# Last feed-forward layer of a four-layer transformer kernel: another order of the last eight work units, and another order inside the last matrix product

## The reference, cut to what matters

```
for i in range(DEPTH):                                   # DEPTH = 6
    x = attn_layer(shift_tokens(x), Wqkv[i], q_scale[i], k_scale[i], Wo[i]) + x
    x = ffn_layer(shift_tokens(x), ln_g[i], ln_b[i], W1[i], b1[i], W2[i], b2[i]) + x

attn_layer: q, k, v = x @ Wqkv; l2-normalise q and k; rotate both; softmax(8 q k^T) v over
            the own window and the one before it; times Wo
ffn_layer:  a, gate = layernorm(x) @ W1 + b1;  (a * gelu(gate)) @ W2 + b2
...
return x + tanh(g_ffn[3]) * _L3_ffn_ref(layernorm(x), ...)
```

## Time and profile before

| | |
|---|---|
| time, median of 3 runs | 4802.01 us (4800.52 to 4803.77) |
| the profiled execution, its own time | 4805.08 us |
| its span in the profile | 4803.7 us |
| mean granted clock of TensorE | 0.989 |
| busy share: PE, DVE, ACT, POOL | 96%, 75%, 65%, 54% |
| last `qkv` matmul of the program ends | about 4700.8 us |
| last matmul of the program ends | about 4798.8 us |

### The profile page before, as it was taken

How to read it: one execution, slowest core, us unless ns; L and a number is a source line. 1 busy time by engine, 2 the same in 40 slices (tenths; PEclk the granted TensorE clock), 3 DMA queues, 4 the chain that set the end, 5 groups by cost and what they waited for, 6 DMA issues and landing times.

```text
span 4803.7 us, 92378 instructions
## 1 busy us (share of the span) xinstructions
PE 4591.3 (96%) x34598; PEld 2927.6 (61%) x34664; DVE 3584.6 (75%) x6388; ACT 3135.8 (65%) x7744; POOL 2594.6 (54%) x2346
## 2 busy tenths in 40 slices
PE   6999999999999999969999999999999999999998
PEld 2333333334444343337788888888888888888886
DVE  4767766766675857858888887888888888887885
ACT  3666566556455556557777777777777777777773
POOL 3322211212121222148888788787888887887873
PEclk8999999999999999989999999999999999999999
DMA  5323323332222323212111111111111111111110
GB/s 121 66 50 62 75 42 60 71 63 47 57 40 60 68 41 74 40 34 54 41 41 35 41 40 36 42 39 37 39 44 39 39 36 41 40 36 38 39 44 31
DMA packets 178924, 233.05 MB, mean 49 GB/s; under 512 B 29648, under 2 KB 121424, under 8 KB 178256
## 3 DMA queue, kind: packets, MB, share of 16 engines
q1 hardware_dynamic: 178480, 227.14, 21.0%
HBM read 150.09 MB, written 32.51 MB: 38 GB/s over the span
## 4 chain that ended last, share of the span: by engine, by line
PE 66%; DVE 12%; ACT 8%; POOL 7%; issue 5%; DMA 1%; SPq 0%; another core or an unknown queue 0%; DVEq 0%; ACTq 0%; POOLq 0%
PE psum L1449 13%; PE psum L1493 11%; PE psum L541 5%; PE psum L527 5%; PE psum L506 5%; PE psum L1535 3%; PE psum L1501 3%; PE psum L488 2%; DVE maxes L731 2%; PE psum L1516 2%; PE psum L1525 2%; POOL stats L1818 2%; PE psum L530 2%; ACT lprobs L1760 2%; PE psum L496 2%
## 5 line engine op out<-in xcount | busy, mean ns | idle before, releaser
L941 ACT ACTIVATE probs<-psum 128x1024 f32<-128x1024 f32 x610 | 621.6, 1023 | 449.2 <-PE psum L527 259.7
L731 DVE TENSOR_REDUCE maxes<-psum 128x1 f32<-128x1024 f32 x512 | 618.1, 1216 | 278.0 <-PE psum L506 274.2
L1818 POOL TENSOR_TENSOR stats<-stats,minus_half 128x8 f32<-128x8 f32 x384 | 687.6, 1791 | 32.0
L1760 ACT ACTIVATE lprobs<-psum,small_stats,stats 128x128 f32<-128x128 f32 x1536 | 690.3, 480 | 20.9 <-DVE small_stats L1649 19.9
L1493 PE MATMUL psum<-wqkv_hi,xs_hi 128*128 128x512 f32 (+1 forms) x1536 | 546.6, 356 | 16.4 <-POOL xs_lo L1805 15.2
L1814 POOL TENSOR_TENSOR lwork<-lwork 128x512 f32<-128x512 f32 x384 | 505.1, 1315 | 74.7 <-DVE lwork L1633 74.6
L527 PE MATMUL psum<-stack 98*128 98x512 bf16 x1536 | 502.8, 384 | 25.9 <-DVE maxes L731 12.2
L1493 PE MATMUL psum<-wqkv_lo,xs_hi 128*128 128x512 f32 (+1 forms) x1536 | 519.3, 338 | 0.0
L1493 PE MATMUL psum<-wqkv_hi,xs_lo 128*128 128x512 f32 (+1 forms) x1536 | 519.0, 338 | 0.0
L506 PE MATMUL psum<-stack 96*128 96x512 bf16 x1536 | 473.3, 385 | 33.2 <-ACT probs L938 10.0
L728 DVE CUSTOM_DVE_ANT_0 psum<-psum,mask_by_query 128x1024 f32<-128x1024 f32 x256 | 314.8, 1231 | 217.8 <-PE psum L506 216.2
(11 more groups left out here) (244 smaller groups left out, 11398.0 us busy)
## 6 DMA issues: line engine op xcount, KB each, us to landing
mixed_vals<-vals SPq DMA_DIRECT2D x672, 64.0 KB, 2.0
stack<-k_parts SPq DMA_DIRECT2D x288, 128.0 KB
staged<-in_quads SPq DMA_DIRECT2D x144, 256.0 KB, 3.0
k_parts<-parts SPq DMA_DIRECT2D x48, 384.0 KB, 2.9
stack<-q_parts SPq DMA_DIRECT2D x288, 64.0 KB
staged<-in_w SPq DMA_DIRECT2D x54, 256.0 KB, 3.0
ctx<-in_ctxT SPq DMA_DIRECT2D x24, 512.0 KB, 5.2
q_parts<-parts SPq DMA_DIRECT2D x24, 384.0 KB, 3.2
```

What stands on the lines that cost most here:

```text
L731: ins = vector.tensor_reduce(to, pair(("M", u)), AX.XY, ALU.max)
L941: scalar.activation(probs[:, i % 6, :, :], pair(("E", u)), ACT.Exp).then_inc(S_["E_act"], 1)
L1760: ins = scalar.activation(pr[:, h, :], scores(u)[:, h % 2, h // 2, :], ACT.Exp, bias=st[:, 4 + h:5 + h], scale=y[:, h:h + 1], accum_out=st ...
L1818: pool_step(gpsimd.tensor_tensor(st[:, 8:16], st[:, 0:8], minus_half[:, :], ALU.pow))
```

## The change

The last four units' places in the last depth change: after (2,2) and (3,2) come (0,2) (1,2) (1,3) (0,3) (3,3) (2,3). Batch 2 has thus all its groups after slot 367 in place of 375, and batch 3 comes last as a whole. By then groups 3 and 2 have made room for groups 1 and 0, so they are loaded again for batch 3: six more `q` chunks and two more `o` chunks. The loads of groups 0 and 1 come eight slots earlier. The feed-forward of batches 1 and 2 gets earlier slots (`norm`, `gates`, `linear`, `second`). Last, `second_matrix` lets batch 3's last `fw` take the hidden tiles 0 to 3 of both halves first and tiles 4 and 5 of both halves at the end.

```diff
--- before.py
+++ after.py
@@ -1203,12 +1203,25 @@
 
 def weights_of(d, g, b):
 
-    return d, 1 if b >= B // 2 and g < 2 else 0, g
-
-
-def last_group(b):
-
-    return 3 - b
+    again = b >= B // 2 and g < 2 or (d, b) == (DEPTH - 1, B - 1)
+    return d, 1 if again else 0, g
+
+
+def last_group(d, b):
+
+    return (3, 2, 1, 2)[b] if d == DEPTH - 1 else 3 - b
+
+
+def second_matrix(d, b, part):
+
+    if (d, b) == (DEPTH - 1, B - 1):
+        return [[(0, i) for i in range(4)], [(1, i) for i in range(4)], [(m, i) for m in range(C) for i in (4, 5)]][part]
+    return [(m, i) for m in range(C) for i in range(HT)][4 * part:4 * part + 4]
+
+
+def done_by(d, b, part):
+
+    return [m for m in range(C) if (m, HT - 1) in second_matrix(d, b, part)]
 
 
 def last_order():
@@ -1224,10 +1237,14 @@
             put(t + n * step, ("lq", name + (j,)))
 
     halves = [((0, 0), (1, 0), (1, 1), (0, 1), (2, 0), (3, 0), (3, 1), (2, 1)), ((2, 2), (3, 2), (3, 3), (2, 3), (0, 2), (1, 2), (1, 3), (0, 3))]
-    units = [(d, g, b) for d in range(DEPTH) for half in halves for g, b in half]
+    ending = ((2, 2), (3, 2), (0, 2), (1, 2), (1, 3), (0, 3), (3, 3), (2, 3))
+    units = [(d, g, b) for d in range(DEPTH) for half in (halves if d < DEPTH - 1 else (halves[0], ending)) for g, b in half]
     for d in range(DEPTH):
         t0 = 64 * d
-        for key, q, o in (((0, 0), -4, 5), ((0, 1), 0, 9), ((0, 2), 12, 21), ((0, 3), 16, 25), ((1, 0), 44, 53), ((1, 1), 48, 57)):
+        again = (((1, 0), 44, 53), ((1, 1), 48, 57))
+        if d == DEPTH - 1:
+            again = (((1, 0), 36, 45), ((1, 1), 40, 49), ((1, 3), 52, 61), ((1, 2), 56, 65))
+        for key, q, o in (((0, 0), -4, 5), ((0, 1), 0, 9), ((0, 2), 12, 21), ((0, 3), 16, 25)) + again:
             load(t0 + q if t0 + q >= 0 else -2, 1 if t0 + q >= 0 else 0, ("q", d) + key, range(3))
             load(t0 + o, 1, ("o", d) + key, range(1))
         for t, j in ((27, 0), (28, 3), (30, 1), (31, 4), (35, 2), (36, 5), (38, 6), (39, 7), (40, 8)):
@@ -1247,8 +1264,10 @@
             t0 = 64 * d + 32 * (b // 2)
             norm = (32, 34, 35, 36, 37, 38, 39) if b % 2 == 0 else (49, 50, 51, 52, 53, 54, 55)
             gates, linear, second = ((40, 44, 48), (41, 45, 50), (49, 52, 53)) if b % 2 == 0 else ((56, 60, 64), (57, 61, 66), (65, 68, 69))
-            if d == DEPTH - 1 and b == B - 2:
-                gates, linear, second = (40, 42, 44), (41, 43, 45), (46, 47, 48)
+            if d == DEPTH - 1 and b == 1:
+                gates, linear, second = (55, 57, 59), (56, 58, 60), (60, 61, 62)
+            elif d == DEPTH - 1 and b == B - 2:
+                norm, gates, linear, second = (27, 29, 30, 31, 32, 33, 33), (34, 36, 38), (35, 37, 39), (40, 41, 43)
             elif d == DEPTH - 1 and b == B - 1:
                 norm, gates, linear, second = (40, 41, 42, 43, 44, 46, 46), (47, 49, 51), (48, 50, 52), (53, 54, 55)
             for t, stage in zip(norm, ("fo", "fa", "fq", "fb", "fy", "fc", "fd")):
@@ -1257,7 +1276,7 @@
                 put(t0 + gates[j], ("hg", (d, b, j)))
                 put(t0 + linear[j], ("ha", (d, b, j)), ("hm", (d, b, j)))
             for i, t in enumerate(second):
-                put(t0 + t, ("fw", (d, b, i)), *([("fx", (d, b, i - 1))] if i else []))
+                put(t0 + t, ("fw", (d, b, i)), *([("fx", (d, b, j)) for j in done_by(d, b, i)]))
             if d == DEPTH - 1:
                 put(t0 + second[0], ("kb", b))
                 put(t0 + second[2] + 1, ("fin", b))
@@ -1340,7 +1359,7 @@
             if stage in ("hg", "ha"):
                 return half_tiles(stage, u)
             if stage == "fw":
-                return [("fw", u[:2], m) for m in range(C) if m == u[2]]
+                return [("fw", u[:2], m) for m in range(C) if (m, 0) in second_matrix(*u)]
             if stage == "wo":
                 return [("wo", u)]
             return [p + (i,) for i in range(ONE.get(stage, 0))]
@@ -1579,7 +1598,7 @@
                 elif stage == "fw":
                     d, b, part = u
                     PE.wait_ge(S_["lq_pool"], loaded(("f", d), HT, HT + 1 + (part > 0)))
-                    for m, i in [(m, i) for m in range(C) for i in range(HT)][4 * part:4 * part + 4]:
+                    for m, i in second_matrix(d, b, part):
                         to = bank(("fw", (d, b), m))
                         w0 = C * 2 * HT * P + i * D + m * P
                         if i == 0:
@@ -1726,7 +1745,7 @@
                     if d:
                         A.wait_ge(S_["fx_dve"], at_("fx", (d - 1, b, C - 1)))
                     if d or b > 1:
-                        A.wait_ge(S_["qkv_pe"], at_("qkv", (d, last_group(b - 2), b - 2, QT - 1) if b > 1 else (d - 1, last_group(b + 2), b + 2, QT - 1)))
+                        A.wait_ge(S_["qkv_pe"], at_("qkv", (d, last_group(d, b - 2), b - 2, QT - 1) if b > 1 else (d - 1, last_group(d - 1, b + 2), b + 2, QT - 1)))
                     for c in range(C):
                         ins = scalar.activation(xs_hi[:, c, b % 2, :], tokens(b, c, c), ACT.Copy)
                     ins.then_inc(S_["xs_act"], 1)
@@ -1821,7 +1840,7 @@
                     gpsimd.tensor_tensor(k, k, bc(st[:, 12:16], 2, LHD), ALU.mult).then_inc(S_["rot_pool"], 1)
                 elif stage == "fo":
                     d, b = u
-                    G.wait_ge(S_["add_dve"], at_("wx", (d, last_group(b), b, C - 1)))
+                    G.wait_ge(S_["add_dve"], at_("wx", (d, last_group(d, b), b, C - 1)))
                     left(work_at, ("n0", u), G)
                     gpsimd.tensor_tensor(buf("n0", u), tokens(b, 0, 0), tokens(b, 1, 1), ALU.add).then_inc(S_["fo_pool"], 1)
                 elif stage == "fq":
```

## The result

The changed kernel takes 4815.23 us (median of 9 runs, 4814.23 to 4817.96). The kernel before took 4803.33 us in the runs beside it (9 runs, 4800.52 to 4804.69). The ratio is 1.0025, with a 95% interval of 1.0016 to 1.0034: slower by 11.9 us. Forecast were 4801.3 us and a range of 4796 to 4809 us. The result is outside the range, on the side that had a chance of 0.04.

A forecast was written before the change was run, and what follows sets the result against it. PE was taken as the bound, with only the tail's 16.8 us of losses to work on. Tail gain -1.7 plus 1.0 us for chunks gave -0.7 us, from 4802.0 to 4801.3 us; range 4796 to 4809 us.

The forecast's parts named there:

- part 4: Eight extra and the earlier chunks on DVE and POOL: 1.0 us lost in slots 356 to 362, 0 in 372 to 385.
- part 2: Attention behind the last projection: PE waits of 1.5, 2.15, 1.0 and 1.0 us, 5.6 us in sum.
- the clock: Tail: one stretch at 1.2 GHz after a gap longer than 3.11 us, costing 2.2 us; before, two cost 4.4 us.
- The bound: Upper limit on PE's loss from the chunk loads: 7.8 us, if POOL's whole addition came out on PE.
- Part 1: Work moved across the last projection: it comes about 14 us later, no gain or loss while PE stays the bound.
- Part 3: Batch 3's layernorm in the tail: PE waits of 0.6, 1.2, 1.2 and 4.3 us, 7.3 us in sum.
- Rival (a): Attention rounds behind the last projection together lower the clock: price 2.2 us, 4803.5 us; chance 0.17.
- This rival: Rival (b): GpSimd and DVE become the bound in slots 356 to 362; up to 7.8 us, 4808.1 us; chance 0.15.
- The second matrix product: Batch 3's last matrix product: PE's 0.65 us wait for tile 4's low part goes, nothing is late next.
- rival (d): One more pair of ACT table changes, with a drain after each load: up to 2.8 us longer, 4804.1 us; chance 0.03.

The follow-up runs named there:

- e3: Changed kernel with batch 0's last step in slot 59 and batch 1's feed-forward one slot later; 4803.64 us.
- e13: Kernel before with batch 1's first gates in slot 55 instead of 56 and first linear matmuls in 56 instead of 57, no chunk moved; 4809.05 us.
- e2: Changed kernel with batch 1's gates, linear matmuls and second matrix one slot later; 4806.36 us.
- the two pairs with and without the spread: Chunks spread so no slot has two: changed kernel 4814.88 us with, 4815.23 without; e7 4802.68 us with, the same kernel without 4801.66.
- e10: e9 with batch 3's first layernorm PE step in slot 40 and batch 2's last products and low parts in slot 43; 4797.64 us.
- e8: Changed kernel with only its end altered: batch 3's layernorm ahead, between parts of batch 2's second matrix, which takes tiles 4 and 5 last; 4813.65 us.
- e9: Changed kernel with all edits together: those of e7 and the end of e8; 4800.19 us.
- e1: Changed kernel with batch 0's last step moved from slot 54 to slot 59; 4811.93 us.
- e7: Changed kernel with batch 0's last step in slot 59, batch 1's gates and linear matmuls one slot later, chunks spread, batch 1's second matrix behind the last projection; 4802.68 us.

## Why the prediction was wrong, step by step

**The failed step is one clause of part 4:** "The loads of slots 372 to 385 lie where PE has batch 1's whole feed-forward to do besides; I take 0 there, and the 7.8 us covers them." With both collisions undone (e3) 11.0 of the 11.9 us are gone, and e13 shows the second of them alone, at 6.5 us, in the kernel before. Not all of the 11.0 belong to this clause: 2.6 us are behind the last projection, where part 2 and the clock were forecast too low. PE did have this work besides, but it was the work that waited. The prediction had followed the queues of SP, DVE and POOL for each moved chunk in slots 356 to 362, found stalls of 0.4 to 2.2 us there, and did not do the same for the chunks in slots 372 to 385. One look at what stands ahead of each new DMA on SP would have shown the output with its wait for DVE, and the feed-forward's table (gates 55, `fd` 55) shows the second collision without any trace.

**The bound was no bound.** 7.8 us was POOL's whole addition in one stretch. The loss came from a wait in SP's queue and from the order on PE, which that figure does not cover: 6.84 us of waiting and 1.9 us of clock are 8.7 us, more than the bound, at a place for which it was not worked out.

**Part 1** (work moved over the last projection costs nothing, 14 us later) was right as arithmetic: 14.7 us in e3, and 14.2 us from slot 374 on. It was wrong as put, "as long as PE stays the bound", because the moved gates are themselves bound to DVE. A moved instruction keeps its inputs' times, and its slack has to be read: before, the low part ended at 4649.52 us and the gates started at 4649.72 us, 0.2 us later:

```profile
4647.76 1.76 DVE L1688 SCALAR_TENSOR_TENSOR xn_lo<-lwork,vecs,xn_hi 128x512 fp32r<-128x512 f32 x2
...
4649.72 0.47 PE L1449 MATMUL psum<-xn_hi,w_hi 128*128 128x512 f32 x1
```

There was no slot to give away.

**Part 2** forecast waits of 1.5, 2.15, 1.0 and 1.0 us, 5.6 in sum. Measured: 2.88, 2.22, none and 0.84 us, 5.9. The first one is 1.79 and 1.78 us in e2 and e3, the kernels with batch 1's feed-forward one slot later. DVE and ACT of the changed kernel show why it is 1.1 us longer there:

```profile
4723.77 1.76 DVE L1738 SCALAR_TENSOR_TENSOR x_back<-x_resid,gates,x_back 128x512 f32<-128x512 f32 x2
...
4726.89 0.60 ACT L1760 ACTIVATE lwork<-psum 128x512 f32<-128x512 f32 x1 [2.11 <-DVE lwork L1652]
```

DVE has batch 1's output additions (`fin`, slot 63) ahead of the last tile's rotation, and ACT waits 2.11 us for that rotation before it gets to the exponentials that PE waits for. In e3, with `fin` a slot later, the same row of ACT waits 0.29 us. This is read from the traces; no run moves that step alone. It is the second output step that the prediction had no term for.

**Part 3** forecast 0.6, 1.2, 1.2 and 4.3 us, 7.3 in sum. Measured: 0.65, 1.35, 1.80 and 4.31 us, 8.1. The chain was right. Two of GpSimd's steps took longer here than in the earlier trace rows: 1.73 in place of 1.27 us, for which PE does not wait, and 1.47 in place of 1.01 us, which is most of what the third wait is over its forecast.

**The clock** was forecast as one stretch worth 2.2 us. There were three: twice 3.4 us between 4725 and 4745 us, with PE busy for 3.1 and 3.4 us of them, and some 10 us around the last two waits, with PE busy for some 5.9. At half speed that costs 1.6 + 1.7 + 3.0 = 6.2 us, taking all of it as lost to PE. Rival (a) came, and the last stretch was longer besides. Losses of the tail: 14.1 + 6.2 = 20.3 us, where the prediction had 15.1 (give or take 3) and the kernel before 16.8. The tail is 3.5 us worse by this working and 3.3 by the spans, not 1.7 us better; the sign was wrong there too. In e3 it is 12.95 us of waits and, by the same working, 4.7 us of clock, 17.7 us: 0.9 us over the kernel before.

**Part 4, slots 356 to 362:** 1.0 us taken. PE is busy for 57.74 of the 60 us in place of 59.50, so 1.8 us show in the trace, and nothing in the medians of the two pairs with and without the spread. This rival, with a chance of 0.15, was not what made the kernel slower. (Three slots there have two chunks, 356, 358 and 360; the prediction counts the last two.)

**The second matrix product:** the wait of 0.65 us is gone, as said.

**The table load** of rival (d): the changed kernel has the extra pair, and work follows the load 1.30 us behind its start:

```profile
4742.75 1.28 ACT L1813 ACT_TABLE_LOAD   x1
4744.05 1.26 ACT L1813 ACTIVATE lwork<-psum,vecs 128x512 f32<-128x512 f32 x2
```

The Trainium skill (ScalarE: Activation LUTs, What ACT_TABLE_LOAD costs) has a drain of about 1380 ns besides. Here too the trace has none, as in the earlier trace rows; the measurement decides.

**The range** took its ends from the costs that I had worked out. The part that I had not worked out had no width in it, and the chance of slower, 0.04, was the chance of a known cost being large. That is the second lesson of the case.

## What to carry to other kernels

For each load that a change puts on a queue, name the instruction in front of it there and what that one waits for; an output that was harmless when nothing stood behind it can hold up a weight. For each matmul group that is moved ahead, compare the end of its last input with its start in the trace of before: the difference, here 0.2 us, is all that it can be moved for nothing. An output step costs its vector engine time as well: look at what it stands in front of there. And here the end's chain of layernorm got shorter when DVE took the mean first (e10), after moving PE's steps alone had left a wait of 3.09 us in it (e8, e9).

## What the runs showed of the hardware

Four things. A wait of 4.21 us on PE, with no other change of work, made the kernel 6.5 us slower: the clock is at 0.66 in the 10 us around its end, so the wait costs half as much again. Nor is a wait's effect on the clock the same each time: a wait of 2.11 us at the first score round of the kernel before was followed by full clock, the like wait of 2.12 us in e13 by 3.4 us at half clock; and behind the same last waits of 1.35, 1.80 and 4.31 us the stretch at half clock is 10.2 us long in the changed kernel and in e3, 6.8 us in e1 and e7. A low part of two 128x512 tiles on DVE takes 1.40, 1.75, 2.41 (the kernel before, 4741.53 us) or 3.47 us; GpSimd does other work beside it each time, and spreading the chunks brought the longest back to 1.40 us. And a chunk of 256 KB that is issued 1 us behind two output transfers of the same size lands 4.3 us after its issue; the median in the kernel before was 3.0 us.
